# Cached key pages turned once and kept in DRAM, values gathered, and two copies moved in ScalarE's order, in a paged attention and LoRA kernel

## What is computed

```python
B, S, HID = (8, 128, 512)
D, HQ, HK = (128, 32, 8)
PAGES, PSIZE, NPP = (64, 32, 16)
...
q, k, v = (einsum('bsd,ed->bse', x, W) for W in (Wq, Wk, Wv))
q, k = rope(rmsnorm(q, q_norm_w), pos), rope(rmsnorm(k, k_norm_w), pos)
kc = k_cache[block_table].reshape(bsz, 512, HK, D)
vc = v_cache[block_table].reshape(bsz, 512, HK, D)
k_all, v_all = concatenate([kc, k], axis=1), concatenate([vc, v], axis=1)
scores = einsum('bqhd,bkhd->bhqk', q, k_all) * SCALE
scores = where(valid, scores, -1e30)
probs = softmax(scores, axis=-1)
o = einsum('bhqk,bkhd->bqhd', probs, v_all)
x = x + einsum('bse,de->bsd', o.reshape(bsz, seqlen, HQ * D), Wo)
```

## Time and profile before

| | |
|---|---|
| median of 3 runs | 1154.88 us (1154.5 to 1155.11) |
| the profiled execution, own time | 1157.93 us |
| its span | 1156.1 us, 23,349 instructions |
| busy: PE, PEld, DVE, ACT, POOL | 99%, 89%, 78%, 80%, 48% of the span |
| granted TensorE clock | 0.999 |
| DMA | 86,733 packets, 98.31 MB, mean 85 GB/s |
| from one step's sum of squares to the next, from step 10 on | 17.06 us |

### The profile page before, as it was taken

How to read it: one execution, slowest core, us unless ns; L and a number is a source line. 1 busy time by engine, 2 the same in 40 slices (tenths; PEclk the granted TensorE clock), 3 DMA queues, 4 the chain that set the end, 5 groups by cost and what they waited for, 6 DMA issues and landing times.

```text
span 1156.1 us, 23349 instructions
## 1 busy us (share of the span) xinstructions
PE 1144.5 (99%) x6960; PEld 1030.6 (89%) x6960; DVE 907.1 (78%) x1883; ACT 927.9 (80%) x1833; POOL 550.3 (48%) x573
## 2 busy tenths in 40 slices
PE   8999999999999999999999999999999999999998
PEld 7888988989999998998998999899899899899997
DVE  8977788777778778777777877877877777777756
ACT  6887888888888888888888888888888888887751
POOL 5766766454444445345445444444534544544400
PEclk9999999999999999999999999999999999999999
DMA  7514322122223223222222322222222222221001
GB/s 244 166 61 138 102 88 96 58 88 80 77 87 93 65 87 90 68 87 88 86 72 87 94 63 87 92 66 88 89 69 86 87 84 71 85 81 53 23 1 73
DMA packets 86733, 98.31 MB, mean 85 GB/s; under 512 B 18768, under 2 KB 65744, under 8 KB 86480
## 3 DMA queue, kind: packets, MB, share of 16 engines
q1 hardware_dynamic: 84016, 90.40, 25.6%
q0 software_dynamic: 2304, 6.29, 1.7%
q10 hardware_dynamic: 288, 0.13, 0.0%
HBM read 90.45 MB, written 6.29 MB: 84 GB/s over the span
## 4 chain that ended last, share of the span: by engine, by line
PE 91%; ACT 3%; DVE 2%; issue 2%; DMA 0%; SPq 0%; POOL 0%; ACTq 0%; DVEq 0%; POOLq 0%
PE ps_s L1386 19%; PE ps_w L327 18%; PE ps_w L328 18%; PE ps_w L329 18%; PE ps_w L1397 9%; PE ps_w L1365 2%; PE ps_w L1406 2%; PE ps_w L1372 2%; ACT ps L679 1%; PE ps_s L1306 1%; DVE m L934 1%; PE ps_s L1340 1%; ACT ps L685 0%; DMA m<-wqkv 0%; DVE o_lo L858 0%
## 5 line engine op out<-in xcount | busy, mean ns | idle before, releaser
L685 ACT ACTIVATE ps<-ps,recip 128x640 f32<-128x640 f32 x256 | 213.3, 834 | 61.9 <-DVE recip L965 61.6
L858 DVE TENSOR_TENSOR pt_lo<-ps_w,pt_hi 128x512 fp32r<-128x512 f32 x322 | 204.4, 684 | 56.3 <-ACT pt_hi L690 53.4
L679 ACT ACTIVATE ps<-ps,negmax 128x640 f32<-128x640 f32 x256 | 213.3, 833 | 25.1 <-DVE negmax L958 24.0
L958 DVE CUSTOM_DVE_ANT_0 ps<-ps_s,mask 128x640 f32<-128x640 f32 x256 | 209.7, 820 | 8.0 <-issue 2.7
L507 POOL TENSOR_SCALAR meansq<-sumsq 128x5 f32<-128x5 f32 x63 | 12.8, 203 | 394.8 <-DVE sumsq L925 392.7
L690 ACT ACTIVATE pt_hi<-ps_w 128x512 fp32r<-128x512 f32 x256 | 139.5, 600 | 73.1 <-PE ps_w L1397 70.2
L327 PE MATMUL ps_w<-w_hi,xt_hi 128*128 128x512 f32 (+1 forms) x496 | 172.1, 347 | 0.0
L328 PE MATMUL ps_w<-w_lo,xt_hi 128*128 128x512 f32 (+1 forms) x496 | 167.3, 337 | 0.0
L329 PE MATMUL ps_w<-w_hi,xt_lo 128*128 128x512 f32 (+1 forms) x496 | 167.3, 337 | 0.0
L1397 PE MATMUL ps_w<-cst,ps 128*128 128x128 f32 x1024 | 133.2, 273 | 0.3 <-DVE qt_lo L858 0.2
L515 POOL TENSOR_TENSOR rot<-u,cos 128x640 f32<-128x640 f32 x63 | 100.6, 1597 | 66.2 <-DVE u L980 66.2
(11 more groups left out here) (186 smaller groups left out, 2640.4 us busy)
## 6 DMA issues: line engine op xcount, KB each, us to landing
kv_raw<-kv SPq DMA_DIRECT2D x832, 32.0 KB, 1.6
xt_hi<-xsplit SPq DMA_DIRECT2D x56, 256.0 KB
xt_lo<-xsplit SPq DMA_DIRECT2D x56, 256.0 KB
w_raw<-wqkv SPq DMA_DIRECT2D x56, 192.0 KB, 3.4
wo_raw<-wo SPq DMA_DIRECT2D x56, 128.0 KB, 3.3
y<-xT SPq DMA_DIRECT2D x8, 256.0 KB, 3.1
y<-x SPq DMA_DIRECT2D x8, 256.0 KB
out<-y SPq DMA_DIRECT2D x8, 256.0 KB, 2.2
```

Of the source, the lines that this page charges most:

```text
L679: nc.scalar.activation(ps[:, h, :], ps[:, h, :], ACT.Exp, bias=negmax[:, s % 2, h:h + 1], scale=-1.0, accum_out=rowsum[:, s % 2, h:h + 1]) ...
L685: nc.scalar.activation(ps[:, h, :], ps[:, h, :], ACT.Copy, scale=recip[:, s % 2, h:h + 1]).then_inc(a_norm, 1)
L858: return nc.vector.tensor_tensor(out_ap, full, hi.bitcast(F32), ALU.subtract)
L958: nc.vector.tensor_tensor_reduce(out=halves(ps[:, h, :]), in0=ps_s[:, h % 2, :, 0:KH], in1=halves(mask[:, s % B, :]), scale=-SCALE, scalar ...
```

## The change

- Heads 0 and 1 (g < KG = 16) stay as they were: keys and values gathered together, keys turned by TensorE in each step.
- In steps 5 to 52 TensorE also turns the cached keys of a later head, in page order and each page once: SyncE loads 256 rows of keys (`k_nat`), TensorE makes two transposes behind the new keys' (`turn_natural_keys`), ScalarE copies the result from PSUM (`k_turned`, behind the new keys' high part), and SyncE stores it in DRAM (`kT`), eight pages of 128 x 32. Eight such steps make a head.
- From g = 16 on SyncE loads turned pages (`key_pages`: sixteen DMAs, each 128 partitions by 32 floats) into the key columns of `kv_raw`. TensorE's KTC transposes fall away there, and the keys' high and low parts are made from SBUF. GpSimd gathers the values alone, by half rows, in every step.
- From g = 16 on the cached keys' high and low parts come ahead of the last exponential and reciprocal, and the split of coming weights behind the new keys' part on ScalarE.
- ScalarE copies the queries of g2 behind O's high part. The turned probabilities are made in the order of heads 1, 0, 2.
- The negative sines are gone: the multiply uses the sines for both halves, and the rotation subtracts.

```diff
 for n in range(B, (HK - 1) * B + 2):
     WO_AT[n + 1] = [n]
 RING = 3
-GATHERED = 12
+TURNED = 2
+KG = TURNED * B
+TPAGES = PAGES // B
+TT = TPAGES * PSIZE // P
+AHEAD = 3
+TURNS = (1, 0, 2)
 WARM = 24
 
...
 kv_raw = sb("kv_raw", [P, 2, CT, 2 * D])
+k_nat = sb("k_nat", [P, TT, D])
+k_turned = sb("k_turned", [P, TPAGES, PSIZE])
+kT = nc.dram_tensor("kT", (HK * PAGES, D, PSIZE), F32).ap()
...
+def wait_keys(eng, g):
+
+    eng.wait_ge(s_keys[g % 2], 16 * NPP * ((g - KG) // 2 + 1))
+
+def wait_stored(eng, h, tiles):
+
+    eng.wait_ge(s_kstored[h % 2], 16 * (B * ((h - TURNED) // 2) + tiles))
+
+def naturals(s):
+
+    n = s + AHEAD
+    return n if KG - B <= n < (HK - 1) * B else None
+
+def key_cols(g):
+    return kv_raw[:, g % 2, :, 0:D]
+
+def tiles_of(keys):
+    return keys.rearrange("p (t q) -> p t q", t=CT)
+
+def naturals_bank():
+    return ps_s[:, 1, 0, 0:TT * P]
 def bank(unit):
...
+def turn_number(s, h):
+
+    return TURNS.index(h) + 1 if s > 0 and h in TURNS else h + 1
...
         sp.dma_start(wo_raw[:, n % RING, :], src[:, wo_piece(n)]).then_inc(s_woraw[n % RING], 16)
-    def cached_pages(g):
-
-        wait(sp, pe_ktc, g - 2)
-        wait(sp, p_v, g - 2, 2)
-        pages = kv.rearrange("(n s) d -> n s d", s=PSIZE)
+    def natural_keys(s):
+        n = naturals(s)
+        if n is None:
+            return
+        if n > KG - B:
+            sp.wait_ge(pe_nat, n - (KG - B))
+        row = (n + B) * TPAGES * PSIZE
+        sp.dma_start(k_nat[:], kv[row:row + TT * P, 0:D].rearrange("(t p) d -> p t d", t=TT)).then_inc(s_knat, 16)
+
+    def keep_keys(s):
+        n = naturals(s)
+        if n is None:
+            return
+        sp.wait_ge(a_nat, n - (KG - B) + 1)
+        page = (n + B) * TPAGES
+        sp.dma_start(kT[page:page + TPAGES].rearrange("n d s -> d n s"), k_turned[:]).then_inc(s_kstored[(n // B + 1) % 2], 16)
+
+    def key_pages(g):
+
+        wait_stored(sp, g // B, B)
+        wait(sp, d_ktc, g - 2)
         for part in range(PPT):
-            at = slice(part * PSIZE, (part + 1) * PSIZE)
             b = I_BLOCK + g % B * CT
             _, ids = nc.values_load_multi_w_load_instructions(
                 cin[part * PSIZE:part * PSIZE + 1, b:b + CT], engines=[mybir.EngineType.SP], min_val=0, max_val=PAGES - 1,
                 skip_runtime_bounds_check_because="pages of the table are numbered from 0 to PAGES - 1")
             for t in range(CT):
-                sp.dma_start(kv_raw[at, g % 2, t, :], pages[bass.ds(ids[t] + g // B * PAGES, 1)].rearrange("o s d -> (o s) d")
-                             ).then_inc(s_pages[g % 2], 16)
+                sp.dma_start(kv_raw[:, g % 2, t, part * PSIZE:(part + 1) * PSIZE],
+                             kT[bass.ds(ids[t] + g // B * PAGES, 1)].rearrange("o d s -> (o d) s")
+                             ).then_inc(s_keys[g % 2], 16)
     def first_queries(k):
...
             keep_x(2)
             keep_x(3)
             natural_x(0)
+        if s > 0:
+            keep_keys(s - 1)
+        natural_keys(s)
         if s + 1 in W_MID:
             w_load(W_MID[s + 1])
         for n in W_AT.get(s + 1, ()):
...
             wo_load(WO_MID[s + 1])
         for n in WO_AT.get(s + 1, ()):
             wo_load(n)
-        if GATHERED <= s + 2 < G:
-            cached_pages(s + 2)
+        if KG <= s + 2 < G:
+            key_pages(s + 2)
         if B <= s + 4 < G:
             fetch_x(s + 4)
     for b in range(B):
...
-        wait(pool, pe_ktc, g - 2)
+        if g < KG:
+            wait(pool, pe_ktc, g - 2)
         wait(pool, p_v, g - 2, 2)
+        halves_of_rows = kv.rearrange("r (two d) -> (r two) d", two=2)
         for t in range(CT):
-            pool.indirect_dma_start(kv_raw[:, g % 2, t, :], None, kv[:, :],
-                                    bass.IndirectOffsetOnAxis(rows[:, g % B, t:t + 1], 0)
-                                    ).then_inc(s_kv[g % 2], 16)
+            if g < KG:
+                pool.indirect_dma_start(kv_raw[:, g % 2, t, :], None, kv[:, :],
+                                        bass.IndirectOffsetOnAxis(rows[:, g % B, t:t + 1], 0)
+                                        ).then_inc(s_kv[g % 2], 16)
+            else:
+                pool.indirect_dma_start(kv_raw[:, g % 2, t, D:2 * D], None, halves_of_rows,
+                                        bass.IndirectOffsetOnAxis(rows[:, g % B, t:t + 1], 0)
+                                        ).then_inc(s_kv[g % 2], 16)
...
         ang = ps[:, 0, 0:B * HALF].rearrange("p (b d) -> p b d", b=B)
-        nc.scalar.activation(sin[:, :, 0:HALF], ang, ACT.Sin).then_inc(a_sincos, 1)
-
-    def minus_sines():
-
-        act.wait_ge(a_sincos, 1)
-        nc.scalar.activation(sin[:, :, HALF:D], sin[:, :, 0:HALF], ACT.Copy, scale=-1.0).then_inc(a_sincos, 1)
+        nc.scalar.activation(sin[:], ang, ACT.Sin).then_inc(a_sincos, 1)
...
     def cached_keys(g):
-        wait(act, pe_ktc, g)
-        nc.scalar.activation(kt_hi[:, 0:L], bank("KTC"), ACT.Copy).then_inc(a_ktc, 1)
+        if g < KG:
+            wait(act, pe_ktc, g)
+            nc.scalar.activation(kt_hi[:, 0:L], bank("KTC"), ACT.Copy).then_inc(a_ktc, 1)
+        else:
+            wait_keys(act, g)
+            wait(act, pe_s, g - 1, 4)
+            nc.scalar.activation(tiles_of(kt_hi[:, 0:L]), key_cols(g), ACT.Copy).then_inc(a_ktc, 1)
+
+    def natural_keys(s):
+        n = naturals(s)
+        if n is None:
+            return
+        act.wait_ge(pe_nat, n - (KG - B) + 1)
+        if n > KG - B:
+            wait_stored(act, (n - 1) // B + 1, (n - 1) % B + 1)
+        nc.scalar.activation(k_turned[:].rearrange("p n s -> p (n s)"), naturals_bank(), ACT.Copy).then_inc(a_nat, 1)
     def new_keys(g):
         wait(act, pe_ktn, g)
...
             expert_products(2)
         if s == 1:
             first_wo_split(3)
-        if has(g2):
-            queries(g2)
         if has(s) and s >= G - HB + 1:
             final_turn(s - (G - HB + 1))
         if has(s):
...
             wait(act, pe_y, s - 2)
             nc.scalar.activation(o_hi[:], bank("O"), ACT.Copy).then_inc(a_o, 1)
+        if has(g2):
+            queries(g2)
         if has(s):
             values(s)
-            probs(s, 0)
-            probs(s, 1)
-            probs(s, 2)
+            for h in TURNS:
+                probs(s, h)
             if s in W_MID:
                 w_split(W_MID[s])
             if s in WO_MID:
                 wo_split(WO_MID[s])
+            if KG <= g1 < G:
+                cached_keys(g1)
             exps(s, 3)
             norm(s, 3)
-        for n in W_AT.get(s, ()):
-            w_split(n)
+        if g1 < KG:
+            for n in W_AT.get(s, ()):
+                w_split(n)
         if has(g1):
             turned_queries(g1)
-            cached_keys(g1)
+            if g1 < KG:
+                cached_keys(g1)
             new_keys(g1)
+        natural_keys(s)
+        if g1 >= KG:
+            for n in W_AT.get(s, ()):
+                w_split(n)
         for unit in ("QT", "KTC", "KTN"):
             turn_x(s, unit)
         if has(s):
...
         wait(dve, p_rot, g - 2, 2)
-        nc.vector.tensor_tensor(m2[:], u[:], sin[:, g % B, :].unsqueeze(1).to_broadcast([P, NH, D]),
+        nc.vector.tensor_tensor(m2[:].rearrange("p h (t d) -> p (h t) d", t=2),
+                                u[:].rearrange("p h (t d) -> p (h t) d", t=2),
+                                sin[:, g % B, :].unsqueeze(1).to_broadcast([P, 2 * NH, HALF]),
                                 ALU.mult).then_inc(d_m2, 1)
     def turned_queries(g):
...
         wait(dve, a_ktc, g)
-        low(kt_lo[:, 0:L], bank("KTC"), kt_hi[:, 0:L]).then_inc(d_ktc, 1)
+        if g < KG:
+            low(kt_lo[:, 0:L], bank("KTC"), kt_hi[:, 0:L]).then_inc(d_ktc, 1)
+        else:
+            low(tiles_of(kt_lo[:, 0:L]), key_cols(g), tiles_of(kt_hi[:, 0:L])).then_inc(d_ktc, 1)
     def new_keys(g):
         wait(dve, a_ktn, g)
...
             largest(4)
         if has(s):
             rowmax(s, 3)
-            probs(s, 0)
-            probs(s, 1)
-            probs(s, 2)
+            for h in TURNS:
+                probs(s, h)
+            if KG <= g1 < G:
+                cached_keys(g1)
             over_sum(s, 3)
         for c in MASK_AT.get(s, ()):
             masks(c, c + 1)
...
+    def turn_natural_keys(s):
+        n = naturals(s)
+        if n is None:
+            return
+        pe.wait_ge(s_knat, 16 * (n - (KG - B) + 1))
+        wait(pe, d_max, s, 4)
+        for t in range(TT):
+            last = nc.tensor.transpose(naturals_bank()[:, t * P:(t + 1) * P], k_nat[:, t, :], ident)
+        last.then_inc(pe_nat, 1)
+
     def scores(s, h):
+        if h == 1 and s > 0 and naturals(s - 1) is not None:
+            pe.wait_ge(a_nat, naturals(s - 1) - (KG - B) + 1)
         if h == 0:
             wait(pe, d_qt, s)
             wait(pe, d_ktc, s)
...
         if has(s):
             scores(s, 3)
-            turn_probs(s, 0)
```

(16 more changed lines are left out.)

36 lines of the change are left out of this document (20 added, 16 removed).

## The result

The changed kernel takes 1157.5 us (median of 15 runs, 1157.13 to 1158.25) against 1154.92 for the kernel before on the same chip (15 runs): a ratio of 1.0023, with an interval of 1.0015 to 1.0031.

What follows compares the result with a forecast made beforehand. TensorE was taken to bound the kernel, with the chain from O to T3 0.36 us behind. Terms 0 + 2.2 + 1.3 = +3.5 us took the median from 1154.88 to 1158.4 us, range 1146 to 1169.

Steps and rivals of the forecast that it cites:

- The sum: Whole kernel: 0 in steps 15 to 62, +2.2 natural transposes, +1.3 head 0's block, together +3.5 us.
- Natural transposes in steps 5 to 14: TensorE, steps 5 to 14: two added transposes make each step 0.22 us longer, +2.2 us.
- Head 0's block waits for the queries' copy: TensorE's early transposes: waits 0.09 us (0 to 0.13) for ScalarE's moved copy, paid in steps 1 to 14, 1.3 us.
- The chain from O to T3: O's high part to T3, head 3's transpose block: 0.36 us room gone; steps 15 to 62 gain zero, within 4.8 us.
- the count of transposes: TensorE's own work: steps 15 to 52 get 0.22 us shorter, steps 53 to 62 0.44; -10.6 us in all.
- TensorE keeps its gain: Rival, chance 0.28: O-to-T3 chain 0.13 us or more shorter, TensorE asks last; 1144.3 to 1150, about 1147.5 us.
- Gathers at nothing: GpSimd's value gathers in every step cost nothing, bound 3 us; as a rival (0.18) 3 to 10 us more.
- DMA: Settled steps: 34 to 62 ns per 128-byte piece, share 68 to 99%, holds; rival that it sets the step, 0.10.
- `kt_lo` from SBUF: VectorE's low part of cached keys from two SBUF operands: 0.68 us; up to 0.7 more on top of GpSimd.
- The sine product: VectorE's multiply by the sine: its new broadcast, in pairs of 64, costs 0.82 us as before.

Runs made afterwards that it cites:

- experiment 12: The kernel before with only GpSimd's gathers held until TensorE has finished the output product; 1154.95 us, ratio 0.9999.
- Experiment 10: Changed kernel with queries' copy back ahead of exponential 2 and GpSimd's gathers held until the output product is finished; 1147.93 us, ratio 0.9938.
- experiment 6: Changed kernel with queries' copy back ahead of exponential 2, without gathering values from the third head on; 1152.07 us, ratio 0.9957.
- experiment 9: Changed kernel with queries' copy back ahead of exponential 2, value gathers from the third head on fetching 64 bytes a row, not 512; 1147.27 us, ratio 0.9934.
- experiment 3: Changed kernel with the turned probabilities in the order of heads 1, 2, 0; 1170.1 us, ratio 1.0117.
- experiment 1: Changed kernel with the queries' copy back in its old place, ahead of exponential 2; 1171.95 us, ratio 1.0132.
- experiment 5: The kernel before with GpSimd gathering keys and values by rows to the end, no page loads, nothing turned; 1164.08 us, ratio 1.0058.
- experiment 7: Changed kernel with queries' copy back ahead of exponential 2 and, from the third head on, next step's values gathered ahead of `v_lo`; 1188.56 us, ratio 1.0278.
- experiment 11: Changed kernel with queries' copy back ahead of exponential 2 and gathers held until VectorE has added the output product; 1148.24 us, ratio 0.994.
- experiment 8: Changed kernel as it is, without gathering values from the third head on; 1161.56 us, ratio 1.0037.

## Why the prediction was right, and where it wasn't

**The sum.** Taking the profile of experiment 12, without late signals, for an ordinary execution of before, the changed kernel's steps 1 to 9 take 2.3 us more, steps 10 to 14 another 1.8, and steps 15 to 61 give 1.7 back. With 0.8 us ahead of step 1 and behind step 61, which no term covers, this makes the 3.3 us between the spans (1156.1 and 1152.9); the medians are 2.6 apart. Predicted: +3.5 = 2.2 + 1.3 + 0. So the early steps cost 4.1 and not 3.5, and the settled ones gave 1.7 and not 0: that the sum is nearly right owes something to luck, and so does a chip without late signals.

**Natural transposes in steps 5 to 14: right.** Predicted 0.22 us a step. Experiment 10 has them without the moved copy: 17.26 against 17.05 in steps 10 to 14, +0.21.

**Head 0's block waits for the queries' copy: right, too small.** Predicted 0.09 us (0 to 0.13); the weight loads show 0.17, the chain 0.15, and 17.42 against experiment 10's 17.26 in steps 10 to 14 gives 0.16. I had let the block start the moment the copy ends; it starts 0.11 us later. Over 14 steps the term is about 2.3 us and not 1.3.

**The chain from O to T3 takes TensorE's gain: right.** TensorE's own work in a settled step is 16.83 us, 0.22 under 17.05, as the count of transposes gave (experiments 6, 9, 10). The changed kernel takes 17.02: the move of one 0.49 us copy costs 0.19 of 0.22. My sum for the chain, O high to the end of `qt_lo`, was 7.04 to 7.08 us and it measures 6.98. Where the wait stands I had wrong: head 0's 0.15 to 0.17 comes first and delays TensorE enough for T3 to wait only the remainder, 0.07 at most (0.51 against 0.44). That the chain would do it alone is shown by the late steps of experiment 3, in which head 0's block comes last. Step 55 has no late signal; all twelve early loads run without a wait, T3 waits for `qt_lo`, and the step is still 17.03 us:

```profile
981.75 1.38 PEld L1497 LDWEIGHTS ps_w<-cst,ps 128*128 128x128 f32 x12
```

```profile
988.34 0.63 PE L1497 MATMUL ps_w<-cst,ps 128*128 128x128 f32 x4 [0.24 <-DVE qt_lo L939]
```

From step 53 on, where no natural transposes are left, my count gave TensorE 16.61 us; with the copy back the step is 16.77 (experiments 6, 9, 10). T3 still costs 0.16 there, by experiment 10's chain of waits: a block without a wait takes 0.44.

```profile
1002.25 0.60 PE ps_w L1499 x4
```

The result, 0 taken and -1.7 us measured over the settled steps, is within the 4.8 us allowed. With the copy back, T3 loads 0.13 us after `qt_lo` ends, against 0.11 with it: there too the room is gone or nearly so.

**TensorE keeps its gain (0.28), 1147.5 us.** It didn't happen, but this time can be had: with the copy back and the gathers held, 1147.9 us. Whether shortening the chain is enough, as I had it, is not shown. With the copy back alone the kernel took 1171.95 us (experiment 1), but on a chip with late signals; on one without, it did not run.

**Gathers at nothing: right for the changed kernel where it was timed, wrong as a reason.** The step is 17.00 without them and 17.02 with them. But I argued from GpSimd's free time and from the mean of five steps, 17.11 against 17.06. That mean was of steps of 16.4 and 18.1 us in turn. One of the two long ones is the language biases' work, as I had it: step 8 has 18.12 us in experiment 12 too, without a late signal. The other, step 6 with 18.2, ends in a late one. GpSimd didn't come last there, as I read the earlier trace rows: its 0.94 us of idle time are the wait for the sum of squares, which ended at 127.97, 0.09 us before its first operation. The steps of 18.0 us ahead of them were there to be seen. My bound of 3 us is too low on a chip with late signals: gathers to the end cost the kernel before 6.6 us there (experiment 5), and the neighbouring orders are 8 to 31 us over the kernel before. What the changed kernel takes on such a chip was not measured.

**DMA: the share was far off, the conclusion held.** 12.4 ns for a piece of 128 bytes where 34 to 62 ns were worked out; the share of a settled step is 0.39, not 0.68 to 0.99. The 62 ns came from giving the semaphores' packets no cost and putting all of a slow stretch of issue on the data; the 34 from a slope between 1 KB and 1.6 KB carried down to 128 bytes. The rule of the Trainium skill ("DMA: Bandwidth & Descriptors", Specifications) on pieces under 512 bytes did not decide anything here: 16 page loads of 128-byte pieces took 9.41 us to issue, 9.15 before, and landed in 1.8 us.

**`kt_lo` from SBUF: right.** 0.71 us against 0.68 predicted, since `v_lo` had mostly ended. **The sine product: not foreseen.** It went from 1.68 to 1.99 us, and not by its new form: the same instruction takes 1.70 in experiment 10. It cost nothing here, since `o_lo` behind it still waited for O's high part.

## What to carry to other kernels

Read a stage's steps one by one before taking their mean: 16.4 and 18.1 us in turn are events that hit single steps, not a step of 17.1. When an instruction starts late, look at when the signal it waits for was sent, and by whom, before blaming its engine. When undoing each of several independent moves makes a kernel slower, ask first whether the kernels ran on the same chip: here stretches with the same instructions took 17.2 us a step on one chip and 18.0 on another. And a copy moved from a place with room into the chain that TensorE waits for costs nearly what TensorE had gained, here 0.18 of 0.22 us a step.

## What the runs showed of the hardware

- Beside gathers of 128 rows on GpSimd's queue, signals of TensorE can come late: 1.7 us after the modelled end for one in experiment 1, 1.4 us in experiment 7. The engine that waits for one starts 0.02 or 0.03 us after it, mostly 0.8 to 1.0 us after the issue of the fourth gather ended (a row maximum in experiments 1 and 5, a copy from PSUM in 7). It happens in every profile of two chips and in the profile of the kernel before, and in none of the changed kernel and of experiments 9 to 12. On one chip the settled steps have it with gathers (5) and don't without (6, 8). Whether the size of the rows or the time of the gathers matters was not found, since experiments 9 to 11 ran on another chip.
- The kernel before takes 1155.0 us on two chips and 1157.1 and 1157.5 on two others.
- A VectorE product of two SBUF operands that starts during a GpSimd product ends 0.68 to 0.69 us after GpSimd's does: 594.54 to 596.53 beside a product that ends at 595.85 in the changed kernel, 589.88 to 591.58 beside one that ends at 590.89 in experiment 10. Its 1.99 and 1.70 us are the same 0.7 us of work with a wait in front.
- A packet of 128 bytes took 12.4 ns of an engine (574.5 to 583 us of the changed kernel), one of 1 KB 57.6 ns in the window of the earlier trace rows.
